# A convolution, a quantized gated FFN and its residual on one core: first load of the input made whole, convolution pairs two in a row, the orders of the first tiles rewritten

## What is computed

```python
# grouped convolution (4 groups of 8 channels, 9 taps) plus a term per sample and channel
out = conv(x, weight, padding=4, groups=4)
y = out + einsum('nd,od->no', cond, c_weight)[:, :, None] + bias[None, :, None]

def fake_quant(t, axis):
    s = max(max(abs(t), axis) / 127, 1e-8)
    return clip(round(t / s), -128, 127) * s

def qlinear(v, w):
    return einsum('bsh,oh->bso', fake_quant(v, -1), fake_quant(w, 1))

h = silu(qlinear(y, w_gate)) * qlinear(y, w_up)   # 512 -> 1376
return x + qlinear(h, w_down)                     # 1376 -> 512
```

## Time and profile before

| | us |
|---|---|
| median of 3 runs (lowest to highest) | 287.47 (287.25 to 288.86) |
| the profiled execution, its own time | 288.19 |
| its span, first to last instruction | 286.4 |
| TensorE busy | 275.9 (96%) |
| VectorE / GpSimd / ScalarE busy | 246.5 / 207.3 / 196.8 |
| chain that ended last | TensorE 71%, VectorE 11%, GpSimd 6%, DMA 5%, issue 4% |
| TensorE's granted clock | 1.00 in all slices |

### The profile page before, as it was taken

How to read it: one execution, slowest core, us unless ns; L and a number is a source line. 1 busy time by engine, 2 the same in 40 slices (tenths; PEclk the granted TensorE clock), 3 DMA queues, 4 the chain that set the end, 5 groups by cost and what they waited for, 6 DMA issues and landing times.

```text
span 286.4 us, 5300 instructions
## 1 busy us (share of the span) xinstructions
PE 275.9 (96%) x1843; PEld 154.2 (54%) x1870; DVE 246.5 (86%) x404; ACT 196.8 (69%) x238; POOL 207.3 (72%) x215
## 2 busy tenths in 40 slices
PE   8898899999999999999999999999999999999995
PEld 5887765464446464644444546664444444444443
DVE  0699999999999979899888877789988889988785
ACT  2229999979598767465877755655688886766640
POOL 1379899997949788675788864756578888766623
PEclk9999999999999999999999999999999999999999
DMA  6999932698439996736679996434456663333356
GB/s 198 404 417 418 422 102 55 171 198 218 109 88 260 230 269 158 211 80 177 159 148 356 246 223 182 115 100 77 124 142 160 163 160 105 91 93 95 94 94 208
DMA packets 81433, 52.41 MB, mean 183 GB/s; under 512 B 69632, under 2 KB 70144, under 8 KB 81280
## 3 DMA queue, kind: packets, MB, share of 16 engines
q1 hardware_dynamic: 81408, 52.08, 65.4%
HBM read 26.77 MB, written 8.39 MB: 123 GB/s over the span
## 4 chain that ended last, share of the span: by engine, by line
PE 71%; DVE 11%; POOL 6%; DMA 5%; issue 4%; ACT 1%; SPq 1%; DVEq 0%; POOLq 0%
PE bank L1194 44%; PE bank L1214 21%; PE bank L1096 6%; DVE gu_max L779 4%; POOL sg_mem L511 4%; DMA hq_mem<-w_gate_up 3%; DVE d_max L795 1%; DVE y_part L829 1%; DMA hq_mem<-hq_mem 1%; POOL xo_mem L519 1%; DVE sg_mem L851 1%; POOL yq_mem L492 1%; DVE gu_scale L785 1%; DVE hq_mem L890 1%; DVE h_max L869 1%
## 5 line engine op out<-in xcount | busy, mean ns | idle before, releaser
L1194 PE MATMUL bank<-wgu_t,xq_mem 128*128 128x512 bf16 (+1 forms) x742 | 153.4, 356 | 1.8 <-DVE h_mem L864 0.3
L511 POOL TENSOR_TENSOR sg_mem<-sg_mem,gu_scale_row 128x512 f32<-128x512 f32 (+1 forms) x96 | 111.0, 1162 | 39.5 <-ACT sg_mem L652 39.4
L1194 PEld LDWEIGHTS bank<-wgu_t,xq_mem 128*128 128x128 bf16 x768 | 73.0, 98 | 74.2 <-DVE h_mem L864 6.0
L652 ACT ACTIVATE sg_mem<-sg_mem,x_scale 128x512 f32<-128x512 f32 (+1 forms) x96 | 63.1, 673 | 31.5 <-DVE sg_mem L851 31.1
L1214 PE MATMUL bank<-wd_t,hq_mem 128*128 128x512 bf16 (+1 forms) x340 | 78.3, 379 | 0.7 <-DMA hq_mem<-hq_mem 0.7
L864 DVE SCALAR_TENSOR_TENSOR h_mem<-bank,x_scale,sg_mem 128x512 f32<-128x512 f32 (+1 forms) x96 | 66.0, 691 | 10.0 <-POOL sg_mem L511 8.3
L851 DVE TENSOR_TENSOR sg_mem<-bank,gu_scale_row 128x512 f32<-128x512 f32 (+1 forms) x96 | 59.9, 627 | 13.8 <-PE bank L1194 13.4
L657 ACT ACTIVATE h_mem<-h_mem,h_inv 128x1376 f32<-128x1376 f32 (+1 forms) x32 | 45.1, 1414 | 26.0 <-DVE h_inv L772 25.9
L1214 PEld LDWEIGHTS bank<-wd_t,hq_mem 128*128 128x128 bf16 (+1 forms) x341 | 33.3, 98 | 40.7 <-DMA hq_mem<-hq_mem 1.0
L869 DVE TENSOR_REDUCE h_max<-h_mem 128x1 f32<-128x1376 f32 x32 | 50.3, 1576 | 0.0
L665 ACT ACTIVATE hq_mem<-h_mem 128x1376 bf16<-128x1376 f32 (+1 forms) x32 | 41.8, 1310 | 0.1
(11 more groups left out here) (67 smaller groups left out, 178.3 us busy)
## 6 DMA issues: line engine op xcount, KB each, us to landing
xo_mem<-x SPq DMA_DIRECT2D x24, 256.0 KB, 3.0
out<-xo_mem SPq DMA_DIRECT2D x24, 256.0 KB, 2.2
slab<-x_pairs SPq DMA_DIRECT2D x8, 576.0 KB, 7.2
slab_taps<-x_pairs SPq DMA_DIRECT2D x7, 576.0 KB, 5.9
hq_mem<-w_gate_up SPq DMA_DIRECT2D x7, 512.0 KB, 10.3
slab_taps<-w_down SPq DMA_DIRECT2D x3, 688.0 KB, 13.2
h_mem<-w_gate_up SPq DMA_DIRECT2D x4, 512.0 KB, 15.2
slab_taps<-x SPq DMA_DIRECT2D x1, 2048.0 KB, 9.8
```

The source lines that it names most:

```text
L511: pool.tensor_tensor(s, s, gu_scale_row[:, 1, at:at + n], ALU.mult).then_inc(silu_scaled, 1)
L652: act.activation(s, s, ACT.Silu, scale=x_scale[:, i:i + 1]).then_inc(silu_done, 1)
L1194: last = pe.matmul(bank[n % 2][:, 0:cols], xq_t[:, g, k, P * c:P * (c + 1)], wgu_t[:, m, k, at:at + cols], start=(k == 0), stop=(k == KT - 1))
```

## The change

It has four parts.

1. **First load.** Before, the first load brought the taps of group 0 and 4 of the first pair's 9 blocks (320 KB), and a second, behind the small inputs, the other 5 (320 KB). Now the first load brings taps and all 9 blocks (640 KB), and `conv_pair(0)` waits for it once.
2. **Load order.** The other groups' taps move from ahead of weight block 0 to behind pair 3; pair 5 goes ahead of weight blocks 2 and 3, pair 6 ahead of 4 and 5.
3. **Pairs in the loop.** Pairs 8 and 9 run in a row before tile 7 (9 was at tile 7), 10 and 11 at tile 9 (were at 9 and 11), 12 and 13 at tile 17, 14 and 15 at tile 19 (were at 17 to 20). The second of two uses banks 4 and 5, so `down` of that tile moves behind the tile's last piece, and its `scale_down` behind `multiply_up(i, 1)`. The four spans' two folds and the group's scales are spread over that tile and the next two.
4. **Orders up to tile 6** are written anew on all engines. In the front, the number of empty matmuls rises from 32 to 48, span copies 10 and 11 go ahead of the first weight copies, and pair 5 ahead of the first turned weights.

```diff
         def conv_bank(q):
-            return banks[(6, 7, 4, 5)[q % 4] if q < FRONT else (6, 7)[q % 2]]
+            return banks[(6, 7, 4, 5)[q % 4] if q < FRONT or q >= 2 * SPANS else (6, 7)[q % 2]]
 
         def conv_before(q):
 
-            return q - 4 if q < FRONT + 2 else q - 2
+            return q - 2 if FRONT + 2 <= q < 2 * SPANS + 2 else q - 4
...
-        PAIRS_AT = {7: 9, 9: 10, 11: 11}
-        PAIRS_AT.update({17 + i: 3 * PAIRS + i for i in range(PAIRS)})
+        FOURS_AT = {9: 2 * PAIRS + 2, 17: 3 * PAIRS, 19: 3 * PAIRS + 2}
...
-        LOADS_AT = {7: 10, 9: 11, 11: 12, 13: 13, 15: 14, 17: 15}
+        LOADS_AT = {7: 10, 8: 11, 11: 12, 13: 13, 15: 14, 17: 15}
...
-                sp.dma_start(slab0_taps0[:, 0:BAND + FIRST * N], x_first).then_inc(first_in, 16)
+                sp.dma_start(slab0_taps0[:, 0:BAND + PAIR], x_first).then_inc(pair_in[0], 16)
...
             load_first()
             load_small()
-            load_pair(0)
             load_pair(1)
             load_pair(2)
-            load_other_taps()
             load_w(0)
             load_w(1)
             load_pair(3)
+            load_other_taps()
             load_pair(4)
+            load_pair(5)
             load_w(2)
             load_w(3)
-            load_pair(5)
+            load_pair(6)
             load_w(4)
             load_w(5)
...
                 multiply_up(i, 0)
                 if i < TILES - 1:
+                    if i not in FOURS_AT:
+                        scale_down(i - LAG)
+                    scale_gate(i, 2)
+                for q in spans_at(i, BY_DVE):
+                    add_shift(q)
+                multiply_up(i, 1)
+                if i in FOURS_AT:
                     scale_down(i - LAG)
-                    scale_gate(i, 2)
-                if i in PAIRS_AT:
-                    add_shift(2 * PAIRS_AT[i])
-                multiply_up(i, 1)
-                if i - 1 in PAIRS_AT:
-                    folds([2 * PAIRS_AT[i - 1] + 1])
+                for q in spans_at(i, range(SLOTS))[1:2] + spans_at(i - 1, range(SLOTS))[3:]:
+                    fold_y(q)
+                for q in spans_at(i - 2, range(SLOTS))[3:]:
+                    if q % SPANS == SPANS - 1:
+                        group_scales(q // SPANS)
...
                 gate_or_up(i, 1, 0)
-                if i < TILES - 1:
+                if i in FOURS_AT:
+                    conv_pair(FOURS_AT[i])
+                    conv_pair(FOURS_AT[i] + 1)
+                elif i < TILES - 1:
                     down(i - LAG)
-                if i in PAIRS_AT:
-                    conv_pair(PAIRS_AT[i])
                 gate_or_up(i, 0, 2)
                 gate_or_up(i, 1, 1)
                 if i == TILES - 1:
                     down(i - LAG)
                 gate_or_up(i, 1, 2)
+                if i in FOURS_AT:
+                    down(i - LAG)
```

More of the change, by code:

```diff
@@ L595, in _ @@
                     convert_y(n)
+                for q in spans_at(i, BY_ACT)[1:]:
+                    shift_span(q)
             for i in range(TILES - LAG - 1, TILES - 2):
@@ L698, in _ @@
             copy_gate_up(10)
+            copy_xq(4)
+            round_y(4)
             round_y(5)
-            silu(0, 0)
             copy_xq(5)
@@ L891, in scale_down, with group_scales @@
                                          wd_scale_row[:, :], ALU.mult, ALU.mult).then_inc(down_scaled, 1)
[L893 to L899 removed]
+            def group_scales(g):
+                group_top(g)
+                group_scale(g)
+                group_inverse(g)
             dve.memset(warm_in[:, :], 0.0).then_inc(warm_ready, 1)
@@ L1018, in _ @@
+            multiply_up(5, 1)
+            multiply_up(5, 2)
+            token_top(4)
+            token_top(5)
+            token_scale(4)
+            token_scale(5)
+            token_inverse(4)
+            scale_down(0)
+            token_inverse(5)
+            multiply_up(6, 0)
             multiply_up(6, 1)
             fold_y(17)
+            fold_y(19)
+            scale_down(1)
             scale_down(2)
@@ L1078, in conv_pair @@
                 g, i = divmod(k, PAIRS)
-                if k == 0:
-                    pe.wait_ge(first_in, 16)
-                else:
-                    pe.wait_ge(pair_in[k], 16)
+                pe.wait_ge(pair_in[k], 16)
                 if k == PAIRS:
                     pe.wait_ge(taps_rest_in, 16)
-                if k >= 2:
+                if k == 2 * PAIRS + 1:
+                    pe.wait_ge(xq_copied, len(XQ_USES))
+                    pe.wait_ge(wd_row_copied, 1)
+                elif k >= 2:
                     for q in (2 * k, 2 * k + 1):
                         conv_bank_free(pe, conv_before(q))
+                if k - 1 in FOURS_AT.values():
+                    tile = next(i for i, first in FOURS_AT.items() if first == k - 1)
+                    pe.wait_ge(down_scaled, tile - LAG)
                 for b in range(BLOCKS):
-                    if k == 0 and b == FIRST:
-                        pe.wait_ge(pair_in[0], 16)
                     at = STEP * (b - 1)
@@ L1208, in down @@
                     pe.wait_ge(down_scaled, i - 1)
-                else:
-                    conv_bank_free(pe, SLOTS - 1)
+                for tile, first in [(LAG, 2 * PAIRS)] + list(FOURS_AT.items()):
+                    if i + LAG in (tile, tile + 1):
+                        conv_bank_free(pe, 2 * first + 2 + i % 2)
+                if TILES - 3 <= i:
+                    conv_bank_free(pe, SLOTS - 4 + i % 2)
                 for j in range(JT):
```

294 lines of the change are left out of this document (140 added, 154 removed).

## The result

| | before | changed |
|---|---|---|
| median us (lowest to highest, 4 runs each) | 288.17 (287.25 to 289.03) | 292.62 (290.43 to 292.96) |
| ratio | | 1.0144, 95% interval 1.0107 to 1.018 |
| profiled execution, own time / span | 288.19 / 286.4 | 292.96 / 291.2 |
| VectorE busy | 246.5 | 250.7 |

The changed kernel is **4.45 us slower**. The forecast was 288.4 with a range to 290.3, so the time lies outside it. One of the four runs took 290.43 and the other three 292.6 to 293.0.

What follows compares the result with a forecast made beforehand. TensorE was taken as the bound (busy 275.9 of 286.4 us), its front held by engines preparing weights and spans. Terms +2.0 - 1.0 - 0.4 + 0.3 = +0.9 us on the median 287.47 gave 288.4, range 286.3 to 290.3.

Steps and rivals of the forecast that it cites:

- Tiles 4 to 6: Early loop tiles: VectorE gets added work, so down(2) waits 0.5 us for scale_down(0); +0.3 us, between 0 and +1.5.
- VectorE becomes the bound in tiles 4 to 6: Slower rival: down(2) waits 1.5 us for scale_down(0) instead of 0.3, as VectorE has no reserve; 289.7, chance 0.21.
- The front, +2.0: Up to the product stream: ScalarE and GpSimd run late, stream at 42.3 against 40.34; +2.0 us, bounds +0.6 and +3.0.
- whatever the front loses or gains until that stream starts goes into the end in full: From the stream's start at 40.34 TensorE has unbroken work up to the last tiles, so front changes reach the end whole.
- First load, idle 1.1: Kernel start: whole load lands at 5.5, TensorE idles about 1.1 us, pair 0 starts at 5.5 instead of 4.29; cost 0.
- TensorE's clock rises late: Slower rival at pairs 0 and 1: idle time delays the clock's rise, pair 0 takes 3.8 us; 289.4, chance 0.12.
- Pairs two in a row -1.0: Loop: back-to-back pairs take 4.26 us instead of 4.50, saving 0.24 four times; -1.0 us, bounds 0 and -1.0.
- folds spread -0.4: Tiles 22 to 24: spreading folds removes part of 0.6 us over the plain pace; -0.4 us, between 0 and -0.6.
- Load order: Front: moving 192 KB of taps saves 0.47 us; block 0 lands at 11.7 instead of 12.2, pair 3 starts at 14.4.

Runs made afterwards that it cites:

- experiment 1: Changed kernel, with the scales of group 1 alone made by eight one-column instructions instead of one over 128x8: 288.19 us, ratio 0.9994 to the kernel before.
- Experiment 6: As experiment 1, plus a spare 128x8 reciprocal on the same operands behind the eight one-column instructions: 287.94 us, ratio 0.9985.
- experiment 2: As experiment 1, but with all engines' front orders from the kernel before, under the new load order: 288.05 us, ratio 0.999.
- all columns: All group and gate/up weight scales by one-column instructions: changed kernel 287.57 us, with old front 287.43; kernel before 289.39, with its loop changed 287.63.
- experiment 7: Changed kernel, with GpSimd alone made to wait for the scales of group 1 ahead of scale_silu(4, 2): 287.97 us, ratio 0.9987.
- experiment 4: Kernel before with the loads' part alone, first load whole and new load order: 288.26 us, ratio 0.999.
- experiment 3: Kernel before with the loop's part alone: pairs 10 and 11, 12 and 13, 14 and 15 in a row, folds spread: 287.78 us, ratio 1.0011.
- experiment 5: As experiment 1, plus one spare 128x8 scale instruction whose result nobody uses: median 291.33 us, ratio 1.0104.
- experiment 8: Changed kernel, with every group scale and every gate and up weight scale made by one-column instructions: 287.57 us, ratio 0.9969.

## Why the prediction was wrong

**The step that failed is "Tiles 4 to 6"**, +0.3 with bounds of 0 and +1.5. The stretch from the stream to tile 3 measured +4.0, with the 0.24 that pairs 8 and 9 save already in it. I looked there for a wait of `down(2)` on `scale_down(0)`, from the lengths of VectorE's instructions. In the changed kernel's trace TensorE waits for no `scale_down`. Once the hold-up is removed the stretch has no wait at all and is 0.3 us shorter than before (experiment 1), so that term was 0. What came instead is the hold-up of `group_scale(1)`: 2.5 us of TensorE's wait, and 1.7 of clock in most runs. The row that could have warned me was in the trace before: the same instruction with 0.75 us, against 0.17 in the loop. I priced each moved instruction on its own engine only, and never laid GpSimd's list beside it. In the kernel before the scale fell into the second of two `scale_silu`, in the changed one into the second of four.

The rival "VectorE becomes the bound in tiles 4 to 6" had the place and the side right, and the mechanism wrong; its 289.7 misses by 2.9.

**The front, +2.0.** The parts of it held in the changed kernel's trace: ScalarE idle 2.37 us (forecast 2.4), GpSimd's last block ending at 39.4 (39.7), the stream at 41.75 (42.3). Of the lag of 1.4, 0.4 was a held weight scale again, which the forecast did not have. And the other traces of this front start the stream up to 1.2 us sooner, so that the close match of the last number is partly luck.

What the lag is worth was put too simply: "whatever the front loses or gains until that stream starts goes into the end in full". It holds between executions of one order. Experiment 6 starts its stream 0.77 ahead of experiment 1 and has its output product of tile 3 0.78 ahead. It fails between two orders: in experiment 2, 1.07 us of lead shrank to 0.3, as VectorE was not early too. In the medians the new orders of the front against the old are 288.19 to 288.05, and 287.57 to 287.43 with all columns, so they cost some 0.1. That is not the whole loss ahead of tile 3. Experiments 1, 6 and 7 equal the kernel before, though by the traces they save 0.24 four times and lose 0.15 by the folds (below). So new loads, front and first tiles together must cost some 0.8 us; this is an estimate, and which of them it is stays open (the loads alone measured 0.999).

**First load, idle 1.1.** It was 0.20: the 640 KB landed 3.7 us after issue, in time for a start at 4.56, not 5.5. In the other traces with this load it took 3.4 to 3.7. The Trainium skill's estimate from "DMA: Bandwidth & Descriptors", "Anatomy of one DMA", which I set aside, was nearer (3.5 us, 4.24). I let the second load's 4.3 us speak for the first, although that one stood behind other bytes. The cost forecast for the end, 0, held (experiment 4: 0.999).

**TensorE's clock rises late**: not so. Pair 0's 36 matmuls took 2.42 us where the kernel before had 3.50. In the other traces with the new first load they took 2.23 to 3.38, never the 3.8 of this rival. The clock did cost something, but 60 us later and after a wait of 2.5.

**Pairs two in a row -1.0, folds spread -0.4.** Two pairs do take 4.17 us. The output products of tiles 17 to 20, made in tiles 21 to 24, start 7.19, 7.22 and 7.17 apart, within 0.3 of plain 7.03 as forecast. But before they were 7.03, 7.47 and 7.16, so the three steps together gave only 0.08. Between tiles 3 and 27 I forecast -1.1 (three times 0.24 and the folds), and the trace shows -0.57. The pairs' part of it held and the folds' part failed. By the starts of the matmuls, TensorE was late for VectorE by 0.75 us in all in this stretch of the kernel before, and by 0.91 in the changed one: one large delay (0.43 at 208.68) went, and several of 0.15 to 0.19 came. So the folds are +0.15 in place of -0.4, and -0.72 + 0.15 is the -0.57. The loop's part alone makes no difference that can be measured in the times (experiment 3, ratio 1.0011). On top of the columns it is worth 1.76 us (289.39 to 287.63), but there it mostly takes away what the columns cost the old loop.

**Load order.** Pair 3 started at 14.03 (14.4 forecast), and at 12.84 to 13.62 in the traces of experiments 1, 5, 6 and 7.

## What to carry to other kernels

When a change moves a small VectorE instruction, look at what GpSimd does at that moment. A `tensor_scalar` from SBUF to SBUF over several elements can be shut out until GpSimd's next gap, or with luck until its next instruction. What it costs is then set by GpSimd's run (up to 3.36 us here) and not by its own length (0.16). A record far longer than its like in the same trace (0.75 beside 0.17) is the sign. A one-column form, or a wait in GpSimd's list ahead of a long run, is the cure. The column form has a price: eight take 0.57 us. In the kernel before, where the scales of groups 2 and 3 were not held and VectorE was already last, it made the whole 0.5% slower. So replace only the instructions that are held.

## What the runs showed of the hardware that was not expected

- The 128x8 `tensor_scalar` was held for 3.36 and 2.84 us, over three GpSimd instructions, though GpSimd passed from one to the next twice meanwhile. In other places it got in at such a change: 0.75 us in the kernel before (77.87), with GpSimd's run going on at 78.53. Every held record of the changed kernel ends 0.02 to 0.03 us after the end of a GpSimd record. What decides at which of them is open.
- In the same place a 128x8 `reciprocal` (0.19 us), 128x1 `tensor_scalar`s (eight in 0.57) and `h_mem` products out of PSUM were not held. The Trainium skill, "VectorE: DVE Perf Modes", "What auto-detection actually checks", says that firmware enables the faster modes for an instruction, and that the engine then takes the two-port one if a single source and the destination are in SBUF and their shapes allow it. The held instruction and the products out of PSUM fit that. The reciprocal had the held one's shape and places, so it is the operation that sets it apart. No record shows the mode itself.
- After a TensorE wait of 2.5 us the granted clock fell to the 1.2 GHz level for some 3.5 us (0.83 over 70 to 80) in the changed kernel's trace, and stayed at 1.00 in that of experiment 5 with a wait of the same length. By their mean clock, three of four and two of four executions lost it. It is not bound to this wait: 11 of the 93 executions of the kernel before that ran beside the experiments read 0.993 or 0.994 too, and took 289.7 to 291.4 us, but none of the 44 of experiments 1, 6, 7 and 8. Why one and not the other, no run here shows.
